# A graph layer on one core: source nodes and features loaded apart, each behind the landing of a third scatter

## The reference, cut to what matters

```python
s = s @ W_nl0; v = einsum('nmi,mk->nki', v, W_nl1)
w = relu(edge_feature @ W_fc1) @ W_fc2          # 224 weights for each edge
xs, xv = s[dst], v[dst]                         # gather
tp = concatenate([w0*xs, w3*dot(xv, sh1), w1*xs*sh1, w2*xv, w4*cross(xv, sh1)])
agg = segment_sum(tp, src, num_segments=N) / 32 # scatter-add
out_s = agg_s @ W_out_s + skip_s; out_v = agg_v @ W_out_v + skip_v
return x + concatenate([silu(out_s[:, :64]), sigmoid(out_s[:, 64:])[:, :, None] * out_v])
```

## Time and profile before

| | |
|---|---|
| median of 3 runs | 1414.35 us (1413.16 to 1416.03) |
| the profiled execution's own time | 1413.66 us |
| its span, first to last instruction | 1411.9 us |
| POOL busy | 1072.1 us (76%) |
| PE busy | 965.4 us (68%) |
| DVE busy | 913.6 us (65%) |
| ACT busy | 430.2 us (30%) |
| moved by DMA | 139.60 MB, 99 GB/s |

### The profile page before, as it was taken

How to read it: one execution, slowest core, us unless ns; L and a number is a source line. 1 busy time by engine, 2 the same in 40 slices (tenths; PEclk the granted TensorE clock), 3 DMA queues, 4 the chain that set the end, 5 groups by cost and what they waited for, 6 DMA issues and landing times.

```text
span 1411.9 us, 26567 instructions
## 1 busy us (share of the span) xinstructions
PE 965.4 (68%) x5852; PEld 814.8 (58%) x5852; DVE 913.6 (65%) x3779; ACT 430.2 (30%) x844; POOL 1072.1 (76%) x826
## 2 busy tenths in 40 slices
PE   7125886777776767578657877685767677678935
PEld 5124775666665646466646766564656557567832
DVE  7603886767566667667675767565675667678625
ACT  5002433333323333333323233232333233234302
POOL 1773888888888888888888888888888888887870
PEclk9556988887778878878878788787798877898977
DMA  9522454545455454545454545545545455546556
GB/s 356 137 66 49 81 102 81 101 79 102 82 83 96 81 103 80 99 82 102 81 100 78 104 80 91 90 80 102 80 87 94 81 104 90 91 79 107 54 71 249
DMA packets 123502, 139.60 MB, mean 99 GB/s; under 512 B 34177, under 2 KB 98369, under 8 KB 123394
## 3 DMA queue, kind: packets, MB, share of 16 engines
q0 software_dynamic: 78720, 73.65, 36.6%
q1 hardware_dynamic: 44674, 64.99, 14.7%
HBM read 86.30 MB, written 52.26 MB: 98 GB/s over the span
## 4 chain that ended last, share of the span: by engine, by line
SPq 41%; issue 29%; DMA 13%; POOL 10%; PE 3%; DVE 2%; ACT 1%; another core or an unknown queue 0%; POOLq 0%; DVEq 0%; ACTq 0%
SPq L346 32%; DMA sums<-to_add,add_idx 6%; SPq L341 6%; POOL sums L423 6%; DMA sums<-spare,add_idx 4%; POOL turn_space L405 2%; POOL spare L405 1%; DMA ef<-edge_t 1%; SPq L299 1%; POOL rows L405 1%; SPq L306 1%; SPq L305 1%; DMA sums<-spare 1%; DMA turn_space<-sums 0%; PE t_ps L606 0%
## 5 line engine op out<-in xcount | busy, mean ns | idle before, releaser
L541 PE MATMUL o_ps<-w,pT 128*128 128x96 f32 (+1 forms) x2496 | 367.1, 302 | 80.4 <-ACT pT L666 43.0
L541 PEld LDWEIGHTS o_ps<-w,pT 128*128 128x128 f32 (+1 forms) x2496 | 348.6, 216 | 115.7 <-issue 92.4
L423 POOL DMA_INDIRECT sums<-to_add,add_idx x208 | 333.1, 1601 | 87.0 <-issue 74.6
L423 POOL DMA_INDIRECT sums<-spare,add_idx x204 | 326.2, 1599 | 62.4 <-issue 56.7
L675 ACT ACTIVATE msg<-o_ps 128x448 f32<-128x448 f32 x208 | 113.2, 544 | 501.7 <-remote 272.6
L525 PE MATMUL t_ps<-w,products_space 128*128 128x128 f32 (+1 forms) x1248 | 219.5, 304 | 58.0 <-DVE products_space L874 41.5
L556 PE MATMUL d_ps<-msg,same 128*128 128x192 f32 x824 | 209.4, 386 | 33.9 <-ACT to_add L687 13.2
L666 ACT ACTIVATE pT<-t_ps 128x512 f32<-128x512 f32 (+1 forms) x312 | 186.0, 596 | 144.5 <-remote 65.6
L405 POOL DMA_INDIRECT turn_space<-node_table,to_idx x186 | 185.6, 998 | 56.7 <-issue 50.6
L556 PEld LDWEIGHTS d_ps<-msg,same 128*128 128x128 f32 x824 | 167.4, 233 | 79.0 <-issue 74.3
L525 PEld LDWEIGHTS t_ps<-w,products_space 128*128 128x128 f32 (+1 forms) x1248 | 168.8, 159 | 75.0 <-DVE products_space L874 40.1
(11 more groups left out here) (125 smaller groups left out, 991.5 us busy)
## 6 DMA issues: line engine op xcount, KB each, us to landing
from_row<-nodes_row SPq DMA_DIRECT2D x52, 512.0 KB
ef<-edge_t SPq DMA_DIRECT2D x52, 256.0 KB
turn_space<-node_table SPq DMA_DIRECT2D x768, 0.6 KB
spare<-node_table SPq DMA_DIRECT2D x768, 0.6 KB
sums<-zeros SPq DMA_DIRECT2D x6, 672.0 KB, 9.5
spare<-sums SPq DMA_DIRECT2D x9, 384.0 KB, 8.6
sums<-to_add,add_idx POOLq DMA_INDIRECT x208
sums<-spare,add_idx POOLq DMA_INDIRECT x204
```

What stands on the lines that cost most here:

```text
L423: pool.indirect_dma_start(sums[t], bass.IndirectOffsetOnAxis(ap=add_idx[:, 2 * v + h, j:j + 1], axis=0), to_add[2 * v + h][:, j, :], None, ...
L541: ins = nc.tensor.matmul(o_ps[m][:, base + oc:base + oc + n], pT[c][u % 2][:, cols], w[0:ROWS[c], wc:wc + n], start=(q == 0 and c == 0), s ...
```

## The change

The source nodes of a block are loaded as 16-bit numbers, which halves the bytes of `from_row` to 256 KB. SP issues them, then 16 rows, then the features, then the other 16 rows. From block 4 on, SP waits in front of the source nodes until the third scatter of the first group of block b-4 has landed, and in front of the features until the third scatter of its second group has.

```diff
-ROWS_PER_LOAD = 16
+ROWS_PER_LOAD = ROWS_PER_BLOCK // 2
...
-        from_row = sb("from_row", [P, 2, 2 * GE], I32)
+        from_row = sb("from_row", [P, 2, 2 * GE], I16)
...
+            def third_scatter_landed(b, h):
+
+                if b >= 0:
+                    p = h * J + 2
+                    t = table_of(b, p)
+                    sp.wait_ge(added[t], 16 * scattered(t, b, p + 1))
...
-            def gather_rows(b):
+            def gather_rows(b, h):
 
-                k, r0 = divmod(b * ROWS_PER_BLOCK, P)
+                k, r0 = divmod(b * ROWS_PER_BLOCK + h * ROWS_PER_LOAD, P)
...
             for b in range(BLOCKS):
                 if b + 1 < BLOCKS:
+                    third_scatter_landed(b - LOOP, 0)
                     load_from(b + 1, (b + 1) % 2)
+                gather_rows(b, 0)
                 if b + 2 < BLOCKS:
+                    third_scatter_landed(b - LOOP, 1)
                     load_features(b + 2, b % 2)
-                gather_rows(b)
+                gather_rows(b, 1)
...
-        "nodes_row": np.ascontiguousarray(in_blocks(src).reshape(1, TILES * P)),
+        "nodes_row": np.ascontiguousarray(in_blocks(src).reshape(1, TILES * P).astype(np.int16)),
```

More of the change, by code:

```diff
@@ L20 @@
 I32 = mybir.dt.int32
+I16 = mybir.dt.int16
 P = 128
@@ L339, in gather_rows @@
                     sp.wait_ge(prod_ready, 2 * (g - ROWS_RING) + 2)
[L340 to L347, removed]
+                _, nodes = nc.values_load_multi_w_load_instructions(
+                    by_row_idx[0:1, k * P + r0:k * P + r0 + ROWS_PER_LOAD], engines=[mybir.EngineType.SP],
+                    min_val=0, max_val=NPAD - 1,
+                    skip_runtime_bounds_check_because="the reference itself takes these as numbers of nodes")
+                for n, node in enumerate(nodes):
+                    sp.dma_start(rows[u][r0 + n:r0 + n + 1, BY_ROW_J, SC:CR],
+                                 table[bass.ds(node, 1), :]).then_inc(rows_in[u], 16)
             sp.wait_ge(by_row_in, 16)
```

## The result

The changed kernel takes 1410.07 us at the median of 22 runs (1405.21 to 1416.08), the kernel before 1414.76 us in as many (1409.48 to 1418.22). The ratio is 0.9966, 95% interval 0.9956 to 0.9975: 4.7 us or 0.34% faster. 1409.0 was forecast.

A forecast was written before the change was run, and what follows sets the result against it. POOL, issuing gathers and scatters back to back, was taken as the bound. The terms -3.5, -0.7, -0.3 and -0.8 sum to -5.3 us, for a forecast of 1409.0 us, range 1404.0 to 1415.5.

The forecast's parts named there:

- What bounds the kernel: Whole kernel: POOL, busy 76% of the span, issues gathers and scatters back to back; some 27 us are true waits.
- The waits for a third scatter: SP's loads from block 4: waits passed at once until near the end, 60 to 20 us to spare; priced at nothing.
- the last ten blocks: Sign on SP: no wait for a scatter shows before its last ten blocks.
- Moving the features: SP's order in each block: features issued some 12 us later, covered by POOL's reserve; cost nothing.
- the reserve named: Group 4's sums are copied 16 us before POOL scatters them, a distance growing by 1.1 us a block.
- The load that scatters meet: Mostly behind the last gathers: smaller, split loads let scatters land before they are wanted; -3.5 us, bounds 0 to -3.9.
- the signs: Things the profile would show if right, among them scatters that meet a load landing by 4.6 us.
- no gap behind 1265 but one of about 0.8: Sign in POOL's list, behind the last gathers: no gap over 0.34 us behind 1265 but one of about 0.8.
- Half the bytes at the start: Smaller from_row: -0.7 us in the first 36 us, -0.3 us between 36 and 135 us.
- Less beside POOL's instructions: Main part: a tenth fewer bytes shortens POOL's scatters and gathers; -0.8 us, bounds 0 to -3.0.
- Comparisons on 16-bit numbers: DVE's comparison of 128x128 tiles: narrower input, no new mode, POOL not held up; 0 us.
- The sum: All terms together: -5.3 us, giving a forecast of 1409.0 us, 0.38% faster.

The follow-up runs named there:

- e3_no_wait: The changed kernel without its two waits for a third scatter, against the kernel before on chip 1: ratio 0.9971.
- e9_more_end: The kernel before with a 512 KB copy added behind only the last three loads of source nodes, against the kernel before on chip 3: ratio 1.0040.
- e4_i32: The changed kernel with 32-bit node numbers, so split and waits alone, against the kernel before on chip 2: ratio 0.9989.
- e1_i16: The kernel before with 16-bit node numbers alone, no split and no waits, against the kernel before on chip 1: ratio 0.9984.
- e0_before: The kernel before, unaltered, profiled once more on chip 2, where its median was 1413.41 us.
- e2_split: The kernel before with features moved behind 16 rows, 32-bit numbers and no waits, against the kernel before on chip 1: ratio 0.9994.
- e8_more_middle: The kernel before with a 512 KB copy added behind the source-node loads of blocks 2 to 48, against the kernel before on chip 3: ratio 1.0114.
- e0_after: The changed kernel, unaltered, run again on chip 3 against the kernel before: ratio 0.9919.

## Why the prediction was right, point by point

**What bounds the kernel.** Right in all profiles: POOL issues back to back, and what changes the time is gaps on POOL, the length of its instructions and, between chips, when its first scatter comes.

**The waits for a third scatter, priced at nothing.** Right where the change was measured first: 1.6 us of waiting, none of it seen on POOL. The first of it stands between 1050 and 1100 us (blocks 38 and 39), a little before the last ten blocks that were named. The step used SP's pace on the one chip that it had, 21.89 us for 32 rows. Where they take 14.8 us it fails: SP runs so far ahead that it reaches nearly each block before block b-4's scatters have landed, the waits hold it for 373 us, and the changed kernel gained 0.81% against 0.29% for e3_no_wait on a chip of like speed. The two ratios are from different chips; that the waits on block b-2 gave 0.9962 and 0.9970 on the same two, and that e3_no_wait and e9_more_end, one on each, have the same scatter times, makes it unlikely that the chips made the difference, but that is an argument and not a measurement.

**Moving the features, priced at nothing.** Right, and by the reserve named: group 4's sums were ready 12 us ahead of POOL (15 before, counted from the end of ACT's copy), and no gap appeared early. The shift itself was read too large: the sums came 2.6 us later, not 12. SP's gain on POOL fell from 1.1 to 0.6 us a block (24.7 us against POOL's 25.3).

**The load that scatters meet, priced at -3.5.** That a load behind the last gathers makes POOL wait is right, e9_more_end shows it. The size was less: of the gaps' 4.4 us 2.5 are left in the first profile, -1.9. Over the profiles, 32-bit kernels without added bytes have 4.4, 3.5, 4.5 and 3.1 us of gaps, mean 3.9; 16-bit ones with the loads of the change or before it 2.5, 1.3, 1.7 and 2.1, mean 1.9: -2.0. What goes with the smaller gaps is the number of bytes; the split and the waits on 32-bit numbers (e4_i32) left 4.5 us. What I had wrong is that a load of 256 KB is harmless wherever it falls: the landing was 4.88 us after issue, not 4.5 at most (4.6 in the signs), and two scatters behind it POOL waits already. So the sign "no gap behind 1265 but one of about 0.8" did not come true in the first profile, which has 2.22 and 0.90.

**Half the bytes at the start, -0.7 and -0.3.** The first is right: first gathers at 35.4 to 35.8 us with 16-bit numbers, 36.2 to 36.5 with 32-bit and no added bytes. The second is not shown, and less than the sum of both arrives: the first scatter comes 0.4 us earlier, not 1.0, and e4_i32 with 32-bit numbers has its first scatter at the same 133.1 us.

**Less beside POOL's instructions, -0.8.** Not seen. In the first profile the scatters' sum rose by 3.5 us, 659.3 to 662.8, and the gathers' fell by 2.2: together 1.3 longer, not 0.8 shorter. No run isolates the term.

**Comparisons on 16-bit numbers, 0.** Right: 301 ns against 311 on the mean, 281 against 282 at the median, no new mode, and e1_i16's comparison does not hold POOL up.

**The sum.** -5.3 was forecast and 4.7 us measured, from 22 runs each. The profiled pair differs by 1.3 us only. The gaps (-1.9) and the start (-0.4) account for 2.3 us; between the first scatter and block 45, less the gaps, the two kernels before took 1139.4 and 1139.9 us and the two with split loads 1138.4 and 1139.0, another 1 us at most, from two profiles each. So the total is right, the signs and places are mostly right, and the terms together came out at some 3 us, not 5.3. That the total lies within 0.6 us of the forecast is in part luck.

## What to carry to other kernels

Read POOL's list of DMAs for gaps first: a landing that comes late costs only where the next scatter to the same table follows within it, so a load is dear in a stretch of scatters alone, and beside gathers too once it falls on such a scatter in block after block. A wait that is idle in one profile is not shown to be idle: here the slack in front of it was set by how fast SP could issue, and that differed between chips, 21.9 against 14.8 us for 32 rows. When a kernel's halves run at nearly the same pace, measure on more than one chip before a part is called useless.

## What the runs showed of the hardware

The same program ran 12 to 13 us apart on different chips, and the rows tell where: SP needs 73.54 us for its first 32 row DMAs on one and 14.78 on another, and the first scatter comes at 133.5 or 115 to 116 us. From the first scatter to the end of the last the quick chip is no quicker: less the gaps, 1237.2 us in e0_before and 1241.2 in e9_more_end. I did not find what differs.

An indirect scatter's time on POOL changes between kernels that issue the same scatters, without any wait showing; that it depends on how the other engines' work lies against it is my reading, not shown. With the upstream held at the ring's end by POOL's own landings, scatters have a mean of 1.63 us and gathers 0.99; held by SP's wait on block b-4, 1.60 and 1.00; held on block b-2, 1.62 and 1.01 on chip 3. Most of the difference is in one place. The third scatter of each run of four has a median of 1.75 or 1.76 us in the five profiles of quick chips without a wait for scatters (e1_i16, e2_split, e3_no_wait, e8_more_middle, e9_more_end), and of 1.56 or 1.57 us in the nine others, among them all of the slower chips, with the waits or without. So what goes with the waits on a quick chip is the short scatter that the slower chips show anyway. In e9_more_end the last three scatters of one run look like this, the third of the run being the middle line, against 1.57 us for its like in e0_after:

```profile
641.27 1.69 POOL L428 DMA_INDIRECT sums<-to_add,add_idx  x1 [0.30 <-issue]
643.26 1.74 POOL L428 DMA_INDIRECT sums<-to_add,add_idx  x1 [0.31 <-issue]
645.31 1.55 POOL L428 DMA_INDIRECT sums<-to_add,add_idx  x1 [0.30 <-issue]
```

Which engine's instruction lengthens it stays open. Beside 62 of the 66 third scatters over 1.70 us in e9_more_end (of 90 up to block 45) lies one of DVE's small operations on `key` (L929), though not beside the one shown, and it lies beside 12 of the 20 under 1.62 us too. No run took it away.
